# Sliding-window attention on one core: the mask of whole 32-query groups as four rows of the operand stacks, the rest as 32 by 32 diagonal blocks

## The reference, cut to what matters

```python
qb = q.reshape(B, H, nb, bs, dk)                 # bs = window = 128, nb = 8 blocks
kw = jnp.concatenate([kp[:, :, :-1], kp[:, :, 1:]], axis=3)   # 256 keys: the block before, and this one
scores = jnp.einsum('bhnrd,bhncd->bhnrc', qb, kw) * scale
dist = bs + r - c                                # r: query 0..127, c: key 0..255
valid = (dist >= 0) & (dist <= window) & (key_global >= 0)
scores = jnp.where(valid, scores, finfo.min)
probs = jax.nn.softmax(scores, axis=-1)
out = jnp.einsum('bhnrc,bhncd->bhnrd', probs, vw)
```

## Time and profile before

| | |
|---|---|
| median of 3 runs | 1250.92 us (1247.12 to 1251.68) |
| the profiled execution's own time | 1251.17 us |
| its span | 1249.3 us |
| TensorE products, busy | 1054.5 us, 84% of the span |
| TensorE loads, busy | 720.7 us, 58% |
| VectorE | 920.8 us, 74% |
| ScalarE | 497.3 us, 40% |
| GpSimd | 166.5 us, 13% |
| mean granted TensorE clock | 0.915 of 2.4 GHz |
| chain that ended last | PE 50%, DVE 27%, ACT 10%, DMA 5% |

### The profile page before, as it was taken

One profiled execution on the slowest core, in us unless ns is written; L12 is line 12 of the kernel. 1 busy time (PEld: TensorE's weight loads), 2 busy tenths in 40 slices (PEclk: granted clock), 3 DMA queues, 4 the chain that ended last, 5 costly groups with the idle time before them and its releaser, 6 DMA issues.

```text
span 1249.3 us, 22021 instructions
## 1 busy us (share of the span) xinstructions
PE 1054.5 (84%) x8593; PEld 720.7 (58%) x8600; DVE 920.8 (74%) x2425; ACT 497.3 (40%) x1027; POOL 166.5 (13%) x251
## 2 busy tenths in 40 slices
PE   3689879967998999999989999899989988966567
PEld 2355645544556665766666755676566646744445
DVE  2823277898789778887888778977898688968911
ACT  2034254316443554336532653355442634441122
POOL 2000000040003000400040000300040004010400
PEclk9579879987999999889998999999998989987768
DMA  9823013302420134012510233014400210020000
GB/s 279 155 39 79 12 41 99 61 1 77 98 47 1 43 105 76 7 35 79 93 24 9 78 87 56 1 41 109 78 4 27 80 17 1 18 76 0 1 25 9
DMA packets 93608, 67.69 MB, mean 54 GB/s; under 512 B 47233, under 2 KB 86337, under 8 KB 93505
## 3 DMA queue, kind: packets, MB, share of 16 engines
q1 hardware_dynamic: 88544, 60.75, 21.0%
q10 hardware_dynamic: 4960, 5.54, 1.6%
HBM read 45.55 MB, written 20.32 MB: 53 GB/s over the span
## 4 chain that ended last, share of the span: by engine, by line
PE 50%; DVE 27%; ACT 10%; DMA 5%; SPq 4%; issue 3%; POOL 1%; ACTq 0%; DVEq 0%; POOLq 0%
PE bank L1595 7%; PE bank L1487 5%; PE bank L1740 5%; PE bank L1667 4%; PE bank L1749 4%; PE bank L1575 4%; PE bank L1546 4%; PE bank L1580 3%; PE bank L1692 3%; DVE state L1219 3%; DVE lane_buf L1197 3%; PE bank L1541 2%; DVE state L1211 2%; DVE u_l L1206 2%; DVE mx L1007 2%
## 5 line engine op out<-in xcount | busy, mean ns | idle before, releaser
L699 ACT ACTIVATE probs<-bank 128x512 f32<-128x512 f32 x256 | 152.0, 597 | 194.8 <-PE bank L1580 194.4
L1595 PE MATMUL bank<-probs,v_ext 128*9 128x128 f32 x2048 | 161.4, 278 | 13.8 <-ACT probs L699 7.3
L1007 DVE TENSOR_REDUCE mx<-bank 128x2 f32<-128x320 f32 x256 | 120.9, 487 | 57.8 <-PE bank L1546 52.0
L339 POOL TENSOR_TENSOR lane_buf<-state,q_l 128x128 f32<-128x128 f32 x128 | 79.6, 655 | 349.7 <-DVEq L1226 349.7
L1595 PEld LDWEIGHTS bank<-probs,v_ext 128*9 128x9 f32 x2048 | 83.4, 91 | 55.6 <-issue 20.1
L1740 PE MATMUL bank<-feat_c,wgu 128*128 128x256 f32 (+1 forms) x384 | 95.0, 398 | 21.3 <-DVE hid_c L1268 15.7
L1575 PE MATMUL bank<-tri_mask,identb 128*128 128x512 bf16 x256 | 102.0, 399 | 1.4 <-DMA q_stack<-m_rows 1.4
L1580 PE MATMUL bank<-q_stack,k_stack 128*128 128x128 bf16 x1024 | 101.7, 223 | 0.0
L1541 PE MATMUL bank<-edge_mask,identb 128*128 128x64 bf16 x512 | 62.0, 206 | 46.4 <-DVE mx L1007 32.0
L1580 PEld LDWEIGHTS bank<-q_stack,k_stack 128*128 128x128 bf16 x1024 | 80.9, 100 | 34.0 <-issue 4.3
L1197 DVE TENSOR_TENSOR lane_buf<-state,til 128x128 f32<-128x128 f32 x256 | 84.3, 329 | 17.0 <-POOL lane_buf L586 10.2
(11 more groups left out here) (167 smaller groups left out, 1753.1 us busy)
## 6 DMA issues: line engine op xcount, KB each, us to landing
k_pieces<-conv SPq DMA_DIRECT2D x48, 128.0 KB, 2.3
k_stack<-k_pieces SPq DMA_DIRECT2D x32, 192.0 KB
k_stack<-k_pieces SPq DMA_DIRECT2D x32, 128.0 KB
k_l<-lane_k SPq DMA_DIRECT2D x8, 512.0 KB, 3.7
q_l<-lane_q SPq DMA_DIRECT2D x8, 512.0 KB, 5.7
q_pieces<-conv SPq DMA_DIRECT2D x24, 128.0 KB, 2.1
q_stack<-q_pieces SPq DMA_DIRECT2D x32, 96.0 KB
tok<-in_x SPq DMA_DIRECT2D x8, 256.0 KB, 3.2
```

Source lines behind the costliest of these rows:

```text
L699: act.activation(probs[:, u % 2], score_bank[u % 2][:], ACT.Exp, scale=float(DK) ** -0.5).then_inc(exp_done, 1)
L1007: dve.tensor_reduce(mx[:, g, 2 * v:2 * v + 2], bank[1 + u % 2][:, 0:2 * SPAN].rearrange("p (h k) -> p h k", h=2), AX.X, ALU.max).then_inc( ...
L1595: last = pe.matmul(bank[5][row:row + VE, col:col + W], v_ext[:, b, kb, h, :], probs[:, u % 2, (hp * 2 + kb) * W:(hp * 2 + kb + 1) * W], st ...
```

## The change

In the second pass the mask of 32 queries against 32 keys is one of three: nothing, all, or one of the two triangles on the diagonal of a block of keys. The change writes "all" into the stacks. Row 52 + g of `q_stack` holds -1e30 for the 32 queries of group g and 0 elsewhere, and row 52 + g of `k_stack` holds 1 for those keys that group g as a whole may not see. The product of the stacks then adds -1e30 there. In the first pass the 160 keys of a group never include such a key, and these rows add 0. What is left are the triangles: `scores` now begins with the four products of the stacks, the first of which starts the bank, and adds the mask afterwards, by four products of 32 output rows (keys) and 128 columns (two heads, two blocks of keys, 32 queries).

The rows are written once, at the start, by 16 DMAs of POOL: for each g one into `q_stack` (48 pieces of 64 bytes, from `pad_row` in DRAM) and two for each range of keys into `k_stack` (24 pieces each, copied from its row of ones). They wait for `stack_init`; TensorE waits for all 16 before its first maximum unit. No later transfer writes these rows.

In the first pass the two edges become one product of 2 x 2 x 32 columns. For that the two heads of a unit lie 256 columns apart in their bank and no longer 160, and DVE's maximum reads them there.

The diff:

```diff
--- before.py
+++ after.py
@@ -40,6 +40,7 @@
 SROWS = DK * sum(m for _, m in STACK_ROWS)
 MROW = SROWS
 PADROW = SROWS + 3
+GROUPROW = SROWS + 4
 BIG = 1e30
 LOG_EXP_SET = "natural_log_exp_and_others"
 SILU_SET = "silu_and_others"
@@ -224,6 +225,7 @@
         stacks_in = [sem(f"stacks_in{r}") for r in range(RING)]
         pad_in = [sem(f"pad_in{r}") for r in range(RING)]
         stack_init = sem("stack_init")
+        group_rows = sem("group_rows")
         sq_rstd = sem("sq_rstd")
         scores1 = sem("scores1")
         max_done = sem("max_done")
@@ -532,6 +534,20 @@
             pool.memset(mm_[:], 0.0).then_inc(zeroed, 1)
             pool.memset(state[:, NC_], 0.0).then_inc(zeroed, 1)
 
+            pool.wait_ge(stack_init, 2)
+            for g in range(W // SUB):
+                row = slice(GROUPROW + g, GROUPROW + g + 1)
+                pool.dma_start(q_stack[row, :, :, SUB * g:SUB * (g + 1)].rearrange("p r h t -> p (r h) t"),
+                               a["pad_row"][:, 0:SUB].rearrange("a (o t) -> a o t", o=1)
+                               .broadcast_to([1, RING * HPH, SUB])).then_inc(group_rows, 16)
+                for lo, hi in ((0, SUB * g), (W + SUB * (g + 1), 2 * W)):
+                    for e in range(CHUNK // (2 * W)):
+                        if hi > lo:
+                            pool.dma_start(
+                                k_stack[row, :, :, 2 * W * e + lo:2 * W * e + hi].rearrange("p r c t -> p (r c) t"),
+                                k_stack[MROW:MROW + 1, 0, 0, 0:hi - lo].rearrange("p (o t) -> p o t", o=1)
+                                .broadcast_to([1, RING * KC, hi - lo])).then_inc(group_rows, 16)
+
             pool.sem_clear(gstep)
 
             steps = 0
@@ -1005,7 +1021,7 @@
                 g, v = divmod(u, UPG)
                 dve.wait_ge(scores1, n * N_UNITS + u + 1)
                 dve.tensor_reduce(mx[:, g, 2 * v:2 * v + 2],
-                                  bank[1 + u % 2][:, 0:2 * SPAN].rearrange("p (h k) -> p h k", h=2),
+                                  bank[1 + u % 2][:].rearrange("p (h k) -> p h k", h=2)[:, :, 0:SPAN],
                                   AX.X, ALU.max).then_inc(max_done, 1)
 
             def max_piece(n, g, step, before):
@@ -1535,15 +1551,13 @@
                         pe.wait_ge(rn_ready, n * 2)
                 if n or u >= 2:
                     pe.wait_ge(max_done, n * N_UNITS + u - 1)
-                pb = bank[1 + u % 2][:, 0:2 * SPAN]
-                edges = pb.rearrange("p (h k) -> p h k", h=2)
-                for e in range(2):
-                    pe.matmul(edges[:, :, e * W:e * W + SUB], identb[:],
-                              edge_mask[:, e * SUB:(e + 1) * SUB].rearrange("p (o s) -> p o s", o=1)
-                              .broadcast_to([128, 2, SUB]), start=(e == 0), stop=False, skip_group_check=True)
+                pb = bank[1 + u % 2][:]
+                pe.matmul(pb.rearrange("p (h e t) -> p h e t", h=2, e=2)[:, :, :, 0:SUB], identb[:],
+                          edge_mask[:].rearrange("p (o e t) -> p o e t", o=1, e=2)
+                          .broadcast_to([128, 2, 2, SUB]), start=True, stop=False, skip_group_check=True)
                 for hp in range(2):
                     for s in range(W // SUB):
-                        last = pe.matmul(pb[s * SUB:(s + 1) * SUB, hp * SPAN:(hp + 1) * SPAN],
+                        last = pe.matmul(pb[s * SUB:(s + 1) * SUB, hp * 2 * W:hp * 2 * W + SPAN],
                                          q_stack[:, r, 2 * v + hp, s * SUB:(s + 1) * SUB],
                                          keys_of(r, 2 * v + hp)[:, s * SUB:s * SUB + SPAN],
                                          start=False, stop=True, skip_group_check=True)
@@ -1572,14 +1586,17 @@
                 if u >= 2 or n:
                     pe.wait_ge(exp_done, n * N_UNITS + u - 1)
                 pb = score_bank[u % 2]
-                pe.matmul(pb[:], identb[:], tri_mask[:].rearrange("p (o t) -> p o t", o=1)
-                          .broadcast_to([128, 2, 2 * W]), start=True, stop=False, skip_group_check=True)
                 for hp in range(2):
                     for kb in range(2):
                         at = (hp * 2 + kb) * W
                         last = pe.matmul(pb[:, at:at + W], keys_of(r, 2 * v + hp)[:, kb * W:(kb + 1) * W],
-                                         q_stack[:, r, 2 * v + hp, :], start=False, stop=True,
+                                         q_stack[:, r, 2 * v + hp, :], start=(hp == 0 and kb == 0), stop=False,
                                          skip_group_check=True)
+                for s in range(W // SUB):
+                    rows = slice(s * SUB, (s + 1) * SUB)
+                    last = pe.matmul(pb[rows, :].rearrange("p (h e t) -> p h e t", h=2, e=2)[:, :, :, rows], identb[:, rows],
+                                     tri_mask[:].rearrange("p (o e t) -> p o e t", o=1, e=2)[:, :, :, rows]
+                                     .broadcast_to([128, 2, 2, SUB]), start=False, stop=True, skip_group_check=True)
                 last.then_inc(scores2, 1)
 
             def values(n, u):
@@ -1855,6 +1872,7 @@
             pe.wait_ge(weights_scaled, 1)
             pe.wait_ge(consts_cast, 1)
             pe.wait_ge(stack_init, 2)
+            pe.wait_ge(group_rows, 16 * (5 * W // SUB - 4))
             for u in range(DONE_EARLY * UPG):
                 scores_max(0, u)
             for g in range(DONE_EARLY):
```

## The result

The changed kernel takes 1243.07 us (median of 20 runs, 1234.12 to 1252.84), the kernel before 1249.82 us beside it (20 runs, 1245.57 to 1255.21). The ratio is 0.9947, 95% interval 0.993 to 0.9964: 6.6 us faster, where 15 were forecast. The profiled execution has 1244.26 us, its span 1242.3, 7.0 less than before, at a mean granted clock of 0.905 (before 0.915).

A forecast was written before the change was run, and what follows sets the result against it. DVE was taken to set the pace until step 14 and PE after it, PE throughout the first block; 3.0 + 11.1 + 1.65 - 0.5 = 15.2 us off 1251.17 gave 1236 us, 8-in-10 range 1229 to 1248.

The forecast's parts named there:

- rival D: Second pass: narrow products cost 0.13 or ScalarE or DVE sets the pace; 0.09 us saved a step, 1242 us; chance 0.07.
- The plain step: Second pass, steps without full-width work behind the scores: four narrow products replace one of 512 columns, -0.15 us a step.
- The rival with the four one behind the other: Second pass: four narrow mask products run one after the other, plain step 0.08 us longer, 1262 us; chance 0.06.
- Steps with full-width work: Second pass, steps 6, 8 to 13, 20, and 4 with pairs: switching to narrow and back cancels the saving, 0 us.
- rival C: Around step 14: PE's longer wait for DVE lowers the clock, 12 us lost over six blocks, 1248 us; chance 0.08.
- Blocks 1 to 6: Steps 15 to 19 and 24 to 31 of these blocks: 1.85 us saved in each, 11.1 us together.
- The first block: Block n = 0, PE sets the pace throughout: 21 steps save 0.15 us each, less 0.1, 3.0 us.
- The last block: Block n = 7: 13 steps save 0.15 us each, less 0.3 for ScalarE's copy coming closer, 1.65 us.
- The start: Before the first maximum unit: 16 POOL DMAs at 1.0 us each delay PE by 0.5 us.
- rival A: At the start: the 16 POOL DMAs cost more, 8.5 us delay at 1.5 us each; 1240 to 1251 us; chance 0.17.
- A's second form: At the start: POOL makes no progress while DVE runs, issues run from 50 us, 11.1 us later, 1247 us.
- The edges: First pass, maximum units: one product of 128 columns instead of two of 64 gains 0 us, out of 0 to 5 possible.

The follow-up runs named there:

- e13_mixed20: Changed kernel with 20 dummy products at the start, old wide mask back only in steps with full-width work, small dummies before late maximum units: 0.9913 of the kernel before.
- the first experiment: Changed kernel with 20 dummy products of 32 columns on PE at the start, where it waits for the first stacks: 0.992 of the kernel before.

## Why the prediction was half right

**The time.** 1236 was forecast with 1229 to 1248 around it; 1243 came. The sign held, and 0.53% is hardly over the 0.5% that the text took for the limit. That it fell near rival D's 1242 is luck: the saving of 0.09 us a step that D assumes did not happen. The error is in three terms of the sum, those of the first block, of blocks 1 to 6 and of the last. The step that failed is the same in all three: each multiplies the saving of a step by a number of steps and takes the waits for transfers and the clock as they were, but for 0.1 or 0.3 us. The runs showed in its place a late transfer, a longer wait for the maxima rows and more time at half clock: 3.0 became -0.7 us, 11.1 became 6.0, 1.65 became -0.5.

**The plain step** (-0.15 us): right, to 0.01. Keys, narrow products, values and the step of 0.94 are as written; with one unit 1.36; the doubled products confirm 0.05 to 0.07 us for four. The rival with the four one behind the other is refuted. The Trainium skill's 81 ns for a product of 128 columns in "TensorE: Matmul & The Clock Gate", section "Back-to-back issue gap", does not hold for the products of 32 output rows here, each written to its own 32 rows: four pass in 0.07 us.

**Steps with full-width work** (0): mis-sized. They are up to 0.10 us longer, 0.58 us over the eight of a block, which eats the 0.60 of steps 2, 3, 5 and 7. The prediction had the sum of steps 0 to 14 right (no change) for a reason that was wrong in this kernel: DVE, it said, hides PE's saving. PE had nothing to save. The earlier trace rows gave a hint, PE busy 29.81 of those 31 us and DVE 25.22. Where PE did save there, in e13_mixed20, DVE took back most of it, so the premise itself is right in the main. Hence its wait near step 15, forecast to grow by 0.9 us, did not grow (0.24 us once the packet was away; the growth to 1.27 in the changed kernel fits the forecast by accident), and the mechanism of rival C, drawn from that wait, did not act in the form given.

**Blocks 1 to 6** (11.1 us): right in the attention. Steps 0 to 30 of the first experiment are 12.2 us shorter than before. Of this the changed kernel lost 6, by the packet and by half clock near step 15, one stretch of it without a packet. And 2.6 us of the first experiment's 12.2 go back in the stretches behind, which have 74 us at half clock instead of 61; that the clock is the cause is read from this, not shown.

**The first block** (3.0 us): failed. The gain in steps 14 to 19 and 24 to 30 is there (1.9 us), and is lost to the maxima rows (1.8), which the prediction charged with 0.1, and in steps 0 to 13: the half clock of the start lasts to 80.2 us instead of 76.9, 0.9 us. The earlier trace rows showed 0.35 us of wait at this very point in another block. The prediction took it for a small number; it meant that the step had no slack.

**The last block** (1.65 us): failed, by the trace to the clock. PE waits 4.64 us for DVE before step 15 (4.23), and the half clock lasts 13.7 us instead of 6.8; steps 14 to 17 take 14.4 us instead of 12.6. No run tests this, and these steps vary: 11.9 to 15.0 us in the other kernels with the short pass, 12.0 to 14.0 with the old one.

**The start** (0.5 us): 0.3 in the trace, 0.7 (-1.2 to 2.6) by the run of it alone; rival A is out. An issue takes 0.52 us, not 1.0. The sum had a slip as well: 35.75 + 16 + 3.5 is 55.25, not 54.75, a delay of 1.05 us by its own terms; A's 8.5 is 9.05. A's second form, POOL standing still while DVE runs, is refuted: DVE was busy 13.02 of the 14 us to 50, and the 16 issues were over at 44.27. The Trainium skill's warning in "SBUF — State Buffer", section "Who interferes with whom", that DVE can hold up the descriptors of GpSimd's DMAs, is for certain DVE instructions, among them `tensor_scalar`. Those start at 45.85 us here, behind the last issue, so no run tests it. **The edges** (0): right.

**Rival C** had 0.08 and was the nearest to the truth: the clock did take time, near step 15 in three of the middle blocks and in the last block. It takes time behind the projections too, where the prediction did not look, but before the change as well: these stretches are no longer in the changed kernel (488.5 us against 489.0). What no rival had is the late transfer.

## What to carry to other kernels

A change in the number of an engine's instructions moves its instruction packets against every transfer; in a loop unrolled block by block, a block of nearly a whole number of packets (256 instructions each here) repeats one collision in each block. Where a DMA lands late for no reason of its own, look for a packet of 16,384 bytes beside it, and try 20 dummy products before believing anything else. Next, a wait of PE can cost clock behind it: dummy products that look like waste gained 0.3% (before the change) and 0.5% (with it, one a unit), or nothing (with it, two a unit), and the place to put them is ahead of the wait that precedes a stretch at half clock. And before calling a saving hidden by another engine, compare the steps one by one: the sum of a stretch can stand still because two terms cancel.

## What the runs showed of the hardware

- An instruction packet holds one DMA engine for 0.9 to 2.2 us. A transfer over all of them issued 0.2 to 0.5 us ahead of it lands 0.8 to 1.7 us later than its 1.93, in 17 cases of 17.
- Four products of 32 output rows and 128 columns, each to its own 32 rows, take 0.07 us together; four more 0.05 to 0.07.
- A change from 32-row to full-width products costs about 0.1 us where another follows at once (0.17 us from the first narrow product to the wide one, 580.61 to 580.78, against 0.07 to the values).
- Behind the projections PE waits 1.61 or 1.62 us once in each of blocks 2 to 6 (1.29 or 1.30 us in e13_mixed20). In the eleven kernels without wide dummy products there, 3.4 or 6.8 us at the 1.2 GHz level began 0.2 to 3.5 us after its end, in 55 cases of 55. One product of 512 columns ahead of each of eight units removed this. Waits of 1.2 us elsewhere were followed by it in some cases only.
- The runs of one kernel differ in the same way: of 20 executions of the changed kernel those at a mean clock of 0.917 took 1234 to 1236 us, those at 0.898 to 0.900 1249 to 1253.
